# TensorE's attention step in another order, the normalisation one step earlier, ScalarE's copies in front of its exponential, and a ring of five for values

## The reference, cut to what matters

```python
xn = layernorm(x)
q, k, v = rope(xn @ Wq.T + bq), rope(ctx @ Wk.T + bk), ctx @ Wv.T + bv   # 16 heads
p = softmax(where(mask == 0, -1e9, q @ k.T / sqrt(8)))                   # within a sequence
x = x + tanh(g_xattn) * ((p @ v) @ Wo.T + bo)
xn = layernorm(x)
logits = xn @ Wr + br;  e = argmax(logits);  gate = softmax(logits)[e]   # one expert per row
x = x + tanh(g_ffn) * gate * (gelu(xn @ W1[e] + b1[e]) @ W2[e] + b2[e])
```

## Time and profile before

| | |
|---|---|
| median of three runs | 304.14 us (303.58 to 305.31) |
| profiled execution | 303.86 us |
| its span | 302.0 us |
| mean granted TensorE clock | 0.955 of full |
| busy: PE | 238.8 us, 79% |
| busy: DVE | 191.4 us, 63% |
| busy: POOL | 182.0 us, 60% |
| busy: ACT | 166.5 us, 55% |
| first projection, tile 0 / tile 31 | 10.17 / 173.08 |
| first transpose of an expert tile | 195.70 |
| last product of an expert tile starts | 291.12 |

### The profile page before, as it was taken

How to read it: one execution, slowest core, us unless ns; L and a number is a source line. 1 busy time by engine, 2 the same in 40 slices (tenths; PEclk the granted TensorE clock), 3 DMA queues, 4 the chain that set the end, 5 groups by cost and what they waited for, 6 DMA issues and landing times.

```text
span 302.0 us, 10491 instructions
## 1 busy us (share of the span) xinstructions
PE 238.8 (79%) x3529; PEld 207.8 (69%) x3529; DVE 191.4 (63%) x639; ACT 166.5 (55%) x481; POOL 182.0 (60%) x222
## 2 busy tenths in 40 slices
PE   1358889997998887888889967866676899999960
PEld 1236667876887676677677846755565899999960
DVE  5545858889898889977798684754452444444420
ACT  2145577887877875687786852352512444444410
POOL 7466665659468885488967766036473445555560
PEclk9999999999999999999999995799877999999995
DMA  7711465446454724143521212411134322200100
GB/s 221 218 17 25 103 177 124 125 114 185 108 136 114 200 59 135 25 126 66 137 46 37 47 36 71 109 33 40 59 107 112 100 65 61 74 29 31 37 19 0
DMA packets 58536, 26.63 MB, mean 88 GB/s; under 512 B 38609, under 2 KB 53990, under 8 KB 58485
## 3 DMA queue, kind: packets, MB, share of 16 engines
q1 hardware_dynamic: 55204, 20.15, 27.7%
q0 software_dynamic: 2272, 4.46, 4.4%
q10 hardware_dynamic: 1008, 1.35, 1.5%
HBM read 16.70 MB, written 5.51 MB: 74 GB/s over the span
## 4 chain that ended last, share of the span: by engine, by line
PE 35%; DVE 13%; POOL 13%; issue 12%; ACT 7%; SPq 6%; DMA 5%; another core or an unknown queue 4%; POOLq 1%; DVEq 0%; ACTq 0%
PE ps L745 11%; SPq L406 5%; PE ps L788 4%; DMA kbd<-kT 3%; POOL rot L545 3%; POOL rot L539 3%; POOL rot_s L541 3%; PE ps L728 2%; PE ps L726 2%; PE ps L727 2%; PE ps L803 2%; DVE mx L1212 2%; ACT pr L589 2%; DMA x_all<-in_x 2%
## 5 line engine op out<-in xcount | busy, mean ns | idle before, releaser
L560 POOL DMA_INDIRECT out<-fin,got x39 | 37.7, 967 | 37.5 <-DVE fin L1261 26.4
L1212 DVE TENSOR_REDUCE mx<-ps 128x16 f16<-128x1024 f32 x32 | 39.1, 1222 | 19.1 <-PE ps L803 15.1
L745 PE MATMUL ps<-w_f,hT 128*128 x312 | 46.8, 295 | 0.0
L512 POOL DMA_INDIRECT rows<-x_all,dest_i x32 | 33.3, 1040 | 21.4 <-DVE x_all L1062 14.3
L1261 DVE SCALAR_TENSOR_TENSOR fin<-ps,got 128x128 f32<-128x128 f32 x39 | 13.6, 350 | 46.9 <-PE ps L745 33.1
L788 PE MATMUL ps<-vx,pr 128*64 128x32 f32 x1024 | 37.3, 227 | 4.1 <-DVE on L1147 2.4
L745 PEld LDWEIGHTS ps<-w_f,hT 128*128 128x128 f32 x312 | 39.7, 199 | 0.8
L788 PEld LDWEIGHTS ps<-vx,pr 128*64 128x64 f32 x1024 | 33.8, 142 | 8.0 <-issue 2.9
L589 ACT ACTIVATE pr<-ps 128x1024 f32<-128x1024 f32 x32 | 32.7, 1023 | 8.7 <-PE ps L830 8.2
L539 POOL TENSOR_TENSOR rot<-qk,cf 128x256 f32<-128x256 f32 x32 | 23.5, 734 | 22.1 <-ACT qk L609 16.3
L657 ACT ACTIVATE hT<-ps 128x512 f32<-128x512 f32 x39 | 23.3, 597 | 23.2 <-PE ps L728 16.2
(11 more groups left out here) (156 smaller groups left out, 604.6 us busy)
## 6 DMA issues: line engine op xcount, KB each, us to landing
kbd<-kT SPq DMA_DIRECT2D x128, 32.0 KB
got<-rows SPq DMA_DIRECT2D x39, 72.0 KB
w_f<-in_W_rows SPq DMA_DIRECT2D x8, 256.0 KB, 2.9
w_r<-in_W_last_row SPq DMA_DIRECT2D x8, 256.0 KB, 4.1
w_f<-in_L_ffn_W SPq DMA_DIRECT2D x8, 256.0 KB
x_all<-in_x SPq DMA_DIRECT2D x3, 512.0 KB, 4.7
xt_all<-in_x_t SPq DMA_DIRECT2D x3, 512.0 KB, 4.3
ct_all<-in_ctx SPq DMA_DIRECT2D x3, 512.0 KB, 4.3
```

The source lines that it names most:

```text
L512: pool.indirect_dma_start(out=rows, out_offset=bass.IndirectOffsetOnAxis(ap=dest_i[:, t:t + 1], axis=0), in_=x_all[:, t, :], in_offset=Non ...
L560: pool.indirect_dma_start(out=out_d, out_offset=bass.IndirectOffsetOnAxis(ap=got_i[:, u % GOT, R_ID:R_ID + 1], axis=0), in_=fin[:, u % FRI ...
L745: mm = pe.matmul(o, hT[:, par, c, :], w2_f[:, bass.ds(e, 1), c, :].rearrange("p o n -> p (o n)"), start=False, stop=(c == FC - 1))
L1212: dve.tensor_reduce(mx[:, t % 2, 0:H], ps_s[:, :].rearrange("p (h k) -> p h k", k=S), AX.X, ALU.max).then_inc(mx_done, 1)
```

## The change

RING stays at 4 for keys and queries, and the values get a ring of their own with five places (`VRING`). On PE the output projection of tile i - 5 moves from the end of the step to the place behind the projection; the scores move in front of PV; the transpose of `on` moves from the middle of the next step to the end of its own step (tile i - 4, behind the transposed scores and in front of the transpose of the maxima), and the product for the output bias in step 4 moves in front of it. On DVE the normalisation moves from the head of step t + 5 to the place behind the maximum in step t + 4, and x2 with its statistics from step t + 6 to t + 5. Routing and scatters follow one step earlier. On ACT the copy of the transposed `on` and that of the maxima stand in front of the exponential, and the copy of k in front of the router part. The first three scatters of results change their step a little.

```diff
...
 RING = 4
+VRING = 5
 GOT = 20
...
         kbd = sb("kbd", [P, RING, 2, 2 * NA, 2, S], F16)
-        vx = sb("vx", [P, RING, 2, 8, 32])
+        vx = sb("vx", [P, VRING, 2, 8, 32])
         mx = sb("mx", [P, 2, P], F16)
...
         def out_step(u):
-            return F0 + 5 + u // 2 if u < 3 else min(max(SCATTER_AT) - 2 + u, STEPS - 1)
+            return F0 + 4 + u if u < 2 else min(max(SCATTER_AT) - 1 + u, STEPS - 1)
 
...
 
-        GROUP_AT = {b - 1 + 6: g for g, (a, b) in enumerate(GROUPS)}
+        GROUP_AT = {b - 1 + 5: g for g, (a, b) in enumerate(GROUPS)}
         STATS_AT = {i: (4 + 2 * i, 5 + 2 * i) if i < 4 else (i + 8,) for i in range(T - 8)}
         RSTD_AT = {1: 1, 3: 2, 7: 3, 11: 4, 15: 5, 19: 6, 23: 7}
-        SCATTER_AT = {**{i: 1 for i in (*range(15, 21), *range(22, 32))}, 32: 4, 36: 3, 37: 2, 38: 2, 41: 3, 42: 2}
+        SCATTER_AT = {**{i: 1 for i in (*range(14, 20), *range(21, 32))}, 32: 3, 35: 3, 36: 2, 37: 2, 40: 3, 41: 2}
         EXPERT_AT = {4 + 3 * e: e for e in range(NE)}
...
             def step(i):
+                t = i - 5
+                if live(t):
+                    act.wait_ge(onT_done, t + 1)
+                    wait(act, op_done, t - 1)
+                    act.activation(onT[:, t % 2, :], ps_onT, ACT.Copy).then_inc(onT_ev, 1)
+                t = i - 3
+                if live(t):
+                    act.wait_ge(mxT_done, t + 1)
+                    wait(act, st_done, t - 1)
+                    act.activation(mxT[:, t % 2, :], ps_mx, ACT.Copy).then_inc(mxT_ev, 1)
                 t = i - 4
...
                                    scale=SCALE).then_inc(p_rdy, 1)
-                t = i - 3
-                if live(t):
-                    act.wait_ge(mxT_done, t + 1)
-                    wait(act, st_done, t - 1)
-                    act.activation(mxT[:, t % 2, :], ps_mx, ACT.Copy).then_inc(mxT_ev, 1)
                 u = i - F0
...
                     act.wait_ge(qe_ev, t + 1)
-                    act.activation(x_all[:, t, R_LOGIT:R_LOGIT + NE], ps_lx, ACT.Copy).then_inc(lx_ev, 1)
                     if t == 0:
...
                     act.activation(qk[:, par, D:2 * D], ps_kv[:, 0:D], ACT.Identity, scale=mask_s[:, t:t + 1]).then_inc(k_ev, 1)
+                    act.activation(x_all[:, t, R_LOGIT:R_LOGIT + NE], ps_lx, ACT.Copy).then_inc(lx_ev, 1)
                     if t == 0:
...
                 if live(t):
-                    s = t % RING
-                    wait(act, pv_done, t - RING + 1)
+                    s = t % VRING
+                    wait(act, pv_done, t - VRING + 1)
                     if t == 0:
...
                                            v_ps[64 * b:64 * b + 64, :, hh, :], ACT.Copy).then_inc(v_ev, 1)
-                t = i - 5
-                if live(t):
-                    act.wait_ge(onT_done, t + 1)
-                    wait(act, op_done, t - 1)
-                    act.activation(onT[:, t % 2, :], ps_onT, ACT.Copy).then_inc(onT_ev, 1)
                 if i - 2 in EXPERT_AT:
...
                     pe.matmul(ps_kv[:, 0:D], pick, bk_h[:, :], start=False, stop=True).then_inc(qkv_done, 1)
+                t = i - 5
+                if live(t):
+                    pe.wait_ge(onT_ev, t + 1)
+                    pe.matmul(ps_op, pick, c_h[:, :], start=True, stop=False)
+                    pe.matmul(ps_op, onT[:, t % 2, :], wo_x[:, :], start=False, stop=True).then_inc(op_done, 1)
                 t = i - 1
...
                     mm.then_inc(stk_done, 1)
+                t = i - 2
+                if live(t):
+                    s = t % RING
+                    pe.wait_ge(kbd_ld[s], (t // RING) * 64 + 64)
+                    pe.wait_ge(qT_ev, t + 1)
+                    wait(pe, mx_done, t)
+                    for a in range(NA):
+                        for b in range(2):
+                            mm = pe.matmul(ps_s[S * b:S * b + S, 2 * P * a:2 * P * a + 2 * P], qT[:, s, a, S * b:S * b + S],
+                                           kbd[:, s, :, 2 * a + b, :, :].rearrange("p w h k -> p w (h k)"),
+                                           start=True, stop=True)
+                    mm.then_inc(s_done, 1)
                 t = i - 4
                 if live(t):
-                    s, par = t % RING, t % 2
+                    s, par = t % VRING, t % 2
                     pe.wait_ge(p_rdy, t + 1)
...
                     first_layer(i - F0 - 1)
-                t = i - 2
-                if live(t):
-                    s = t % RING
-                    pe.wait_ge(kbd_ld[s], (t // RING) * 64 + 64)
-                    pe.wait_ge(qT_ev, t + 1)
-                    wait(pe, mx_done, t)
-                    for a in range(NA):
-                        for b in range(2):
-                            mm = pe.matmul(ps_s[S * b:S * b + S, 2 * P * a:2 * P * a + 2 * P], qT[:, s, a, S * b:S * b + S],
-                                           kbd[:, s, :, 2 * a + b, :, :].rearrange("p w h k -> p w (h k)"),
-                                           start=True, stop=True)
-                    mm.then_inc(s_done, 1)
-                t = i - 5
-                if live(t):
-                    if t == 0:
-                        pe.wait_ge(s_cs, 2)
-                    pe.wait_ge(on_done, t + 1)
-                    wait(pe, x2_done, t)
-                    if i - 3 in GROUP_AT:
-                        pe.wait_ge(g_read, GROUP_AT[i - 3] + 1)
-                    pe.transpose(ps_onT, on[:, t % 2, :], ident).then_inc(onT_done, 1)
                 if i == 3:
...
                 if i - 2 in GROUP_AT:
-                    if live(i - 5):
-                        pe.wait_ge(onT_ev, i - 4)
-                    else:
-                        pe.wait_ge(x2_done, T)
+                    pe.wait_ge(x2_done, min(T, i - 4))
                     rank_of(GROUP_AT[i - 2])
-                t = i - 5
-                if live(t):
-                    pe.wait_ge(onT_ev, t + 1)
-                    pe.matmul(ps_op, pick, c_h[:, :], start=True, stop=False)
-                    pe.matmul(ps_op, onT[:, t % 2, :], wo_x[:, :], start=False, stop=True).then_inc(op_done, 1)
+                if i == 4:
+                    pe.wait_ge(s_prep, 5)
+                    pe.wait_ge(s_wow, 2)
+                    pe.wait_ge(s_idw, 1)
+                    pe.matmul(bank[4][:, P:P + QX], c_bc[:, :], id_wr[:, :], start=True, stop=True).then_inc(s_c, 1)
+                t = i - 4
+                if live(t):
+                    if t == 0:
+                        pe.wait_ge(s_cs, 2)
+                    pe.wait_ge(on_done, t + 1)
+                    wait(pe, x2_done, t)
+                    if i - 3 in GROUP_AT:
+                        pe.wait_ge(g_read, GROUP_AT[i - 3] + 1)
+                    pe.transpose(ps_onT, on[:, t % 2, :], ident).then_inc(onT_done, 1)
                 if tile(i - F0):
...
                     pe.transpose(ps_mx, mx[:, t % 2, :], ident_h).then_inc(mxT_done, 1)
-                if i == 4:
-                    pe.wait_ge(s_prep, 5)
-                    pe.wait_ge(s_wow, 2)
-                    pe.wait_ge(s_idw, 1)
-                    pe.matmul(bank[4][:, P:P + QX], c_bc[:, :], id_wr[:, :], start=True, stop=True).then_inc(s_c, 1)
-
             pipeline(step)
...
                                       ).then_inc(f_lo, 1)
-                t = i - 5
-                if live(t):
-                    dve.wait_ge(pv_done, t + 1)
-                    wait(dve, on_done, t - 1)
-                    o_ps = ps_o.rearrange("p (h c) -> p h c", c=16)
-                    dve.reciprocal(rden[:, t % 2, :], o_ps[:, :, HD]).then_inc(rden_done, 1)
-                    dve.wait_ge(rden_done, t + 1)
-                    wait(dve, onT_done, t - 1)
-                    dve.tensor_tensor(on[:, t % 2, :].rearrange("p (h d) -> p h d", d=HD), o_ps[:, :, 0:HD],
-                                      rden[:, t % 2, :].rearrange("p (h o) -> p h o", o=1).broadcast_to([P, H, HD]),
-                                      ALU.mult).then_inc(on_done, 1)
                 t = i
...
                                              in1=w1_h[:, e, :], op0=ALU.mult, op1=ALU.subtract).then_inc(s_w1lo, 1)
-                t = i - 6
+                t = i - 5
                 if live(t):
...
                     route_place(third)
-                t = i - 6
+                t = i - 5
                 if live(t):
...
                                       ).then_inc(mx_done, 1)
+                t = i - 4
+                if live(t):
+                    dve.wait_ge(pv_done, t + 1)
+                    wait(dve, on_done, t - 1)
+                    o_ps = ps_o.rearrange("p (h c) -> p h c", c=16)
+                    dve.reciprocal(rden[:, t % 2, :], o_ps[:, :, HD]).then_inc(rden_done, 1)
+                    dve.wait_ge(rden_done, t + 1)
+                    wait(dve, onT_done, t - 1)
+                    dve.tensor_tensor(on[:, t % 2, :].rearrange("p (h d) -> p h d", d=HD), o_ps[:, :, 0:HD],
```

(2 more changed lines are left out.)

## The result

The changed kernel takes 316.88 us (median of 4 runs, 315.29 to 319.79) against 303.86 for the kernel before beside it (4 runs, 302.93 to 305.31): ratio 1.042 [1.037, 1.048]. The forecast was 317.5. Single executions of a kernel that took over 1.5% longer than its fastest one are left out of the ratios in this document, and the profiled executions of experiments 6 and 11 are of that kind. The profiled execution took 315.5 us, span 313.7, against 303.86 and 302.0. I split the 11.7 us of span by the starts of projections: the projection of step 5 begins at 36.90 (was 35.96, +0.9), that of step 31 at 182.98 (was 173.08; steps 5 to 30 take 146.1 us and took 137.1, +9.0), and the rest takes 130.7 (was 128.9, +1.8).

What follows compares the result with a forecast made beforehand. No single engine bounded the whole span; in attention a loop through PE and DVE did. The first tile's 1.7 us plus 11.9 for steps 5 to 30 made 13.6 on 303.86: 317.5 us, range 305 to 323.

Steps and rivals of the forecast that it cites:

- rival A: Attention steps: PE is the bound at 4.5 us where the maximum starts by 2.3; 300.6 us, chance 0.12.
- The maximum's start: Attention step, projection to DVE's maximum: held by DVE's list, 2.64 us in quiet steps, 3.19 with expert weights.
- Maximum to projection: Attention step, maximum's start to next projection: PE waits for the moved normalisation, 2.2 us in place of 1.38.
- Routing: Routing steps in attention: present length plus 0.8 us; DVE's routing operations taken at 12.7 us, between 7.3 and 14.6.
- Key blocks: PE's scores in attention: key blocks land late for the earlier scores, costing 2.0 us, mostly hidden by DVE being late.
- rival C: PE's clock falls to half inside attention, about 4 us per 10 us stretch; 321.5 us, chance 0.15.
- my own case: Attention steps 5 to 30: the normalisation behind the maximum lengthens the PE-DVE loop; 311 to 321 us, chance 0.54.
- The first tile: Start of step 5: PE's transpose for tile 0 waits for c_h, moving the projection to 37.7, 1.7 us later.
- ACT: ACT's list in attention: exponential behind two copies makes k 0.26 us and kT some 0.35 us later.
- The pass into the experts: Steps 31 to 36, where attention meets the expert tiles: counted as nothing, -3 to +3 us.
- Rival B: Attention: PE stalls on key blocks before the scores, 0.3 us in 20 steps; 311.5 us, chance 0.13.
- the rule weighed: Routing on DVE: two-SBUF-input operations and GpSimd operations lock each other out, leaving the sum anywhere from 312 to 319 us.

Runs made afterwards that it cites:

- experiments 6: Changed kernel with the scores back behind PV and DVE's reciprocal and product in front of the maximum; 295.55 us, ratio 1.024.
- 11: Kernel 10 with the three DMAs of each expert's weights issued by ACT in place of SP; 317.27 us, no interval.
- Experiments 2: Changed kernel with the scores put back behind PV, the normalisation staying behind the maximum; 319.74 us, ratio 1.049.
- 6 to 8: The middle one: changed kernel with two small chained reciprocals on DVE between the normalisation's reciprocal and product; 315.67 us, ratio 1.091.
- kernel 3: Changed kernel with ACT's exponential ahead of the copies of the transposed outputs and maxima; 317.91 us, ratio 1.043.
- kernels 5: Kernel before the change with the scores in front of PV and five places for values; 293.31 us, ratio 1.015.
- 10: Kernel before with scores in front of PV, five places for values, and ACT's maxima copy before the exponential, k before the router part; ratio 1.008, median 308.48 us.
- 12: Kernel before the change with the three DMAs of each expert's weights issued by ACT in place of SP; 311.64 us, ratio 1.017.
- kernel 8: Changed kernel with two small chained reciprocals on DVE behind the normalising product, in front of the casts; 300.66 us, ratio 1.039.

## Why the prediction was right

The mechanism was the one forecast, except in the quiet steps (rival A below), and signs named for it are there: PE held in front of the transpose of `on` by DVE's product (15 waits, in 26 steps), the maximum starting without idle time on DVE (4.3 us left in 32), steps with weights longer than quiet ones (5.0 to 5.3 where neither routing nor key blocks add to them, against 4.47), a later step 5. Experiments 2 and 6 to 8 show it: the loss goes up and down with what stands between the maximum and the transpose of `on`. By the steps of the prediction:

- *The maximum's start.* Forecast 2.64 in a quiet step and 3.19 with a weight; measured 2.49 and 3.07. x2 came right behind q's scaling (53.10), as the output projection was early enough. Over the 26 steps the sum forecast (149.0 less 26 x 2.2) 91.8 us up to the maximum; they took 92.4. This half was right, with errors of both signs in it: quiet steps shorter, key blocks longer.
- *Maximum to projection, the mis-sized term.* Forecast 2.2, measured 1.97 to 2.00 at full clock. DVE begins the reciprocal 0.08 before the maximum's recorded end (55.38 against 55.46), not 0.04 behind it, and the signal to PE took 0.06, not 0.12. 26 times 0.22 are 5.7 us too many. Falls of the clock gave back about 2 us of the error: step 26 has 3.79 there.
- *Routing.* Forecast the present length plus 0.8. The steps 10 to 13, 17 to 21 and 24 to 27 grew by 8.4 us together, 0.64 each, some 2.9 of it by the clock (next point but one). All others together grew by 0.6 us: what quiet steps win, those with weights lose.
- *Key blocks.* Forecast 2.0 us for the new order; PE stood 3.1 us longer than before. (Three issues of 0.65 us and 1.98 are 3.9, not the 4.3 of the working.) In the changed kernel part of that lies in front of a maximum that DVE would have delayed anyway.
- *The clock, rival C.* It came true beside my own case. Against kernel 3, which has the same lists on PE and DVE and the full clock in these steps, step 20 is 0.85 us longer and steps 26 and 27 2.1: an estimate of 2.9 us for 13.7 us at half, less than the 4 per 10 us that I gave it. It is not what makes the 4%: kernel 3, with 6.8 us at half in attention, has the same ratio. The rows do not bear out that the longer routing steps bring PE to it, as I had it: the fall at 153.40 came right behind the stall of step 25, but out of a stretch with 24.97 us busy of 30.40.
- *The first tile.* Forecast 1.7 us, measured 0.9. c_h was ready at 36.62, 0.2 us earlier than in the kernel before, where I had it later.
- *ACT.* Forecast k 0.26 and kT 0.35 later. They weren't: in steps 8 and 25 k's copy began 1.43 and 1.44 us after the projection and kT's 1.86 (1.51 and 1.90 before, in step 17). In step 8 the two copies begin at 0.14 and 0.31 us of the step, so the exponential is through at 1.5, and ACT waits for DVE's q anyway. This step of the working failed; its weight was small, since I had put only 2.0 us on all late key blocks.
- *The pass into the experts.* Forecast 0, -3 to +3; measured +1.8, with 34 us at half clock where it was some 20. No experiment separates this.
- *Rival A* (PE the bound, steps of 4.5, 300.6) fell for the whole, but it is what happened in the quiet steps, which I had forecast at 4.85. PE came to the transpose at 4.22 us of step 8 (the rival had 4.25), the product was ready at 4.18, and the step took 4.47, the length of PE's own work. The rival's bound, a maximum that starts by 2.3 us, was 0.2 too early, since only 1.69 us pass from there to the product's end (54.26 to 55.95), not 1.84. Five steps are of this kind (5, 8, 14, 28, 29: 4.47 to 4.65); two of them still wait 0.1 to 0.2 for the product.
- *Rival B* (key blocks decide, 311.5) is wrong for the change but fits the order: kernels 5 and 10, which have no normalisation behind the maximum, still lose 0.8 to 1.5%, with 9.5 to 11.3 us of waits on key blocks (2.2 in the kernel before). That these waits are the loss is argued from their size; the two kernels meant to test it (11 and 12) changed ACT's list too. I had priced the order without that cover at up to 8 us and used 2. In no version run here did the turned order gain.

The sum: +0.9 for +1.7, +9.0 for +11.9, +1.8 for 0; 11.7 us for 13.6. So the profiled execution (315.5) is 2.0 below the forecast. The median lies 1.4 above that execution and so only 0.6 from the forecast; this closeness is luck: the errors of the sum (0.8 and 2.9 too much, 1.8 too little) partly cancel, and the profiled execution was one of the two shorter ones.

On the rule weighed: the routing line that had 176/205/1687 ns now has (ns min/median/max, first and last start, forms)
```profile
L1000 DVE SCALAR_TENSOR_TENSOR cand<-ldif,cf x5: 183/319/906, 76.0 to 221.5; 128x56 f32<-128x56 f32 x3, 128x48 f32<-128x48 f32 x1, 128x40 f32<-128x40 f32 x1
```
and another on 56 elements, with both inputs in SBUF, took from 149.91 to 151.00 in step 25 (1.09 us) while POOL rotated from 149.50 and 150.18, the second time to 150.92. The Trainium skill (SBUF — State Buffer, section on the two separate sides) has a DVE operation with two SBUF inputs and a GpSimd operation that reads SBUF lock each other out for a whole instruction. The rows agree. Which routing operation is hit differs between the two kernels, so the price of routing could be bounded but not told.

## What to carry to other kernels

When a loop passes through several in-order engines, cut each step at the instruction where the engines meet (here the maximum) and sum both halves: where that engine arrives last, an instruction costs its full time in each round if it stands between that point and what the other engine waits for, and next to nothing just behind. Look also at what the waiting engine still has to do itself, as in the quiet step here. A reordering that starts one engine earlier gains only until the next engine's list ends, so read the idle time before the meeting point in all kinds of step (0.85, 0.19 and 0 us here), not in the quiet one. And if the move shortens the distance from a transfer's start to its use, price that by itself: here the waits for it grew from 2.2 to 11.3 us in the best turned order, and the gain was gone.

## What the runs showed of the hardware that I had not expected

- A DVE reciprocal on 128x16 that waits for nothing lengthened the loop by 0.11 us; two that wait for each other by 0.57, 0.28 each. By these two, over half of the 0.28 goes with the wait on the instruction before.
- The same program took 288.88 us on one chip and 303.86 to 305.43 in the three other sets of runs, with the first attention step alike to 0.02 us. The difference lies behind attention: kernel 8, on the fast chip, and the changed kernel begin step 31 at 181.44 and 182.98, and then take 117.9 and 130.7 us. They differ in the clock too, which stood at half for some 14 us in the one and for 34 in the other (without the last 9 us of each); how much of the difference it makes was not tested.
- Three DMA issues in ACT's list took from 65.87 to 67.45 us, and the exponential behind them began at 67.55 (experiment 12).
- TensorE's clock fell to half in attention, for 3.4 us or more, in every profile but that of the kernel before: for 3.4 and 10.2 us in the change, twice for 3.4 us in kernel 3 (from 86.8 and 117.5), which has the same lists on PE and DVE. The ratios of these two kernels don't differ.
